# First attention of a two-layer kernel: the swap of k's halves issued by ScalarE, and another order of work on TensorE

## The chip, the core and the metric

The kernel runs on one core of a Trainium2 chip. The metric is the device time of one execution in microseconds (us), lower is better. The kernel before takes 1952.88 us (median of three runs, 1952.42 to 1953.05).

## What is computed

The reference is a two-layer transformer over 32 samples of 256 tokens with 128 channels. Only the first attention is touched by the change:

```python
h = _layernorm(x, axis=-1) * (1 + ca) + sa
x = x + ga * _L0_attn_ref(h, norm_w, Wq, Wkv, Wout, q_gamma, k_gamma)
...
# inside _L0_attn_ref, for each sample: 16 query heads and 8 key heads of 64
x = _rmsnorm(tokens, norm_w)
q = (x @ Wq).reshape(b, n, QH, DH).transpose(0, 2, 1, 3)
kv = x @ Wkv
...
q = _mh_rmsnorm(q, q_gamma)
k = _mh_rmsnorm(k, k_gamma)
sim = jnp.einsum('bhgid,bhjd->bhgij', q, k)
sim = jnp.tanh(sim / SOFTCLAMP) * SOFTCLAMP
sim = sim * DH ** (-0.5)
sim = jnp.where(causal, neg, sim)
attn = jax.nn.softmax(sim, axis=-1)
out = jnp.einsum('bhgij,bhjd->bhid', attn, v)
```

Behind it come a mixture of experts, a second attention and a gated network. They are the same in both kernels.

## The kernel before, in words

`build` runs five stages one after another: `setup`, `attention0`, `moe`, `attention1`, `mlp`. `attention0` is one loop over samples, written as a software pipeline: iteration n holds the attention of sample n, the normalising of q and k of sample n+1, the projections of sample n+2 and the layer norm of sample n+3. Each of the five engines has its own list of calls for an iteration, in an order written out by hand, and engines meet only through semaphores that count finished calls (`s_qg` counts the `dve_gain` calls, six for a sample; `s_ks` the copies of k, two; `s_k2` the landed swaps of k, 16 for a transfer). An engine takes its calls strictly in the written order, so a call that waits holds up all that stand behind it.

The calls of one sample on TensorE (PE), with the names that the rows use:

- **projections** `pe_project_qk` (L448), six calls m = 0 to 5 of 512 columns in f32, m = 2 and 5 giving k; `pe_values` (L411), two calls of the same size. Three PSUM banks `pW[0..2]` are shared by projections, values, transposes and the output projection; the tables `QK_BANK`, `QT_BANK`, `KT_BANK` and others say which call writes which bank, and the waits at the head of a call say whose reading of that bank must be over.
- **turns of k and q** `pe_turn_k` (L466, t = 0, 1) and `pe_turn_q` (L490, i = 0 to 3), eight f16 transposes each.
- **score products** `pe_score` (L513), 48 calls in f16, 256 columns each, twelve for each of four groups g of heads. q and k are split into a high and a low f16 half that lie in the two halves of the partitions. Odd calls use `k2`, which is k with its halves swapped, even calls use `k1`. `pe_score(n, 0, 0)` waits for `s_k2`; the call m = 0 of each group also waits until the tanh of the group before has read the score banks `pS` (`s_th`).
- **weighing** `pe_weigh` (L533, L535), 48 calls of 66 columns in f32, twelve for each group. The first of a group waits for the mask (`s_mk`).
- **heads back** `pe_heads_back` (L551, eight f32 transposes), **output projection** `pe_out_project` (L563, four calls of 256 columns in f32), `pe_out_back` (L581) and `pe_transpose_x` (L396), two transposes each.

An f32 product is two MATMUL records of the trace, an f16 product or a transpose is one.

On ScalarE (ACT): `act_tanh` and `act_exp` (L1001, L1009) for each group, `act_square_qk` (L965) for each of the six projections, `act_take_k` (L985) two copies of k out of PSUM into `k1`, and smaller calls. On VectorE (DVE): `dve_gain` (L794), which multiplies a projection out of PSUM by gamma and so frees its bank, `dve_sums`, `dve_factors`, `dve_norm`, `dve_outputs`, `dve_take_q` (L874). On GpSimd (POOL): the causal masks (L1083), sums and two low halves. For each projection, square on ACT comes first and gain on DVE behind it (`dve_gain` waits for `s_sq`).

SyncE (SP) issues all transfers. In iteration n of its own loop it waits until both copies of k of sample n are there, and issues the two transfers that swap the halves (L378, L379) and behind them the load of a row of modulations for sample n+3 (L365). In iteration 1 it also issues all the loads of later weights.

Of the kernel before, what the change touches and what calls it, by code (L numbers as in the profile page):

```python
# [14 lines left out]
P = 128  # L15
# [281 lines left out]
def attention0(nc, c, weights, later, following):  # L297
# [3 lines left out]
    with ExitStack() as ctx:  # L301
# [87 lines left out]
        def pe_transpose_x(pe, n, t):  # L389
            if not 0 <= n < B:  # L390
                return
            if t == 0:
                pe.wait_ge(s_hm, 2 * n + 2)
                if n >= 1:
                    pe.wait_ge(s_qg, 6 * n - 2)
# [4 lines left out]
        def pe_values(pe, n, t):  # L400
# [3 lines left out]
            if t == 0:  # L404
                if n + 1 < B:
                    pe.wait_ge(s_qg, 6 * n + 7)
                else:
                    pe.wait_ge(s_qg, 6 * n + 4)
            else:
                pe.wait_ge(s_va, 2 * n + 1)  # L410
            pe.matmul(pW[V_BANK[t]][:, :], hT[n % 2][:, t * P:(t + 1) * P], wkv[:, KW:2 * KW], start=True, stop=True).then_inc(s_v, 1)  # L411

        def pe_project_qk(pe, n, m):
# [3 lines left out]
            if m == 0:  # L417
                pe.wait_ge(s_hT, n + 1)
            elif m == 1:
                if n >= 2:  # L420
                    pe.wait_ge(s_qs, 4 * n - 5)
                elif n >= 1:
                    pe.wait_ge(s_qg, 6 * n - 1)
            elif m == 2:
                if n >= 1:
# [3 lines left out]
            elif m == 3:  # L429
                if n >= 1:  # L430
                    pe.wait_ge(s_qs, 4 * n - 3)
                else:
                    pe.wait_ge(s_qg, 6 * n + 3)
            elif m == 4:
                if n >= 1:
                    pe.wait_ge(s_qs, 4 * n - 2)
                else:
                    pe.wait_ge(s_qg, 6 * n + 2)
# [11 lines left out]
        def pe_turn_k(pe, n, t):  # L450
# [3 lines left out]
            if t == 0:  # L454
                if n + 1 < B:
                    pe.wait_ge(s_qg, 6 * n + 9)
                else:
                    pe.wait_ge(s_va, 2 * n + 2)
            else:
                if n + 1 < B:  # L460
                    pe.wait_ge(s_qg, 6 * n + 8)
                else:
                    pe.wait_ge(s_qs, 4 * n - 1)
# [5 lines left out]
        def pe_turn_q(pe, n, i):  # L469
# [4 lines left out]
            if i == 0:  # L474
                pe.wait_ge(s_ks, 2 * n + 1)
            elif i == 1:
                pe.wait_ge(s_ks, 2 * n + 2)
            elif i == 2:
                if n + 1 < B:
                    pe.wait_ge(s_qg, 6 * n + 11)  # L480
                else:
                    pe.wait_ge(s_qs, 4 * n + 2)
            else:
                if n + 1 < B:
                    pe.wait_ge(s_qg, 6 * n + 12)
                else:
                    pe.wait_ge(s_st, 3 * n - 5)
# [51 lines left out]
        def pe_heads_back(pe, n, t, j):  # L539
# [3 lines left out]
            if j == 0:  # L543
                if t == 0:
                    if n + 1 < B:
                        pe.wait_ge(s_qs, 4 * n + 8)
                    else:
                        pe.wait_ge(s_st, 3 * n - 2)
                else:
                    pe.wait_ge(s_at, 2 * n + 1)  # L550
# [4 lines left out]
        def pe_out_project(pe, n, j):  # L555
            if not 0 <= n < B:
                return
            if j == 0:
# [3 lines left out]
                pe.wait_ge(s_at, 2 * n + 2)  # L562
# [12 lines left out]
        def pe_out_back(pe, n, t):  # L575
            if not 0 <= n < B:
                return
            if t == 0:
                pe.wait_ge(s_og, n + 1)
                pe.wait_ge(s_og, n + 1)  # L580
# [5 lines left out]
        def _(pe):  # L586
            pe_spread_first_rows(pe)
            pe.wait_ge(s_prep, 2)
            for n in range(-3, B + 2):
                for m in range(4, 8):  # L590
                    pe_score(pe, n, 1, m)
                    pe_weigh(pe, n - 1, 3, m + 1)
                pe_score(pe, n, 1, 8)
                pe_score(pe, n, 1, 9)
                pe_weigh(pe, n - 1, 3, 9)
                pe_score(pe, n, 1, 10)
                pe_score(pe, n, 1, 11)
                pe_weigh(pe, n - 1, 3, 10)
                pe_turn_q(pe, n, 3)
                pe_weigh(pe, n - 1, 3, 11)  # L600
                pe_values(pe, n + 1, 0)
                pe_weigh(pe, n, 0, 0)
                pe_project_qk(pe, n + 2, 1)
                pe_weigh(pe, n, 0, 1)
                pe_score(pe, n, 2, 0)
                pe_weigh(pe, n, 0, 2)
                pe_score(pe, n, 2, 1)
                pe_weigh(pe, n, 0, 3)
                pe_score(pe, n, 2, 2)
                pe_heads_back(pe, n - 1, 0, 0)  # L610
                pe_heads_back(pe, n - 1, 0, 1)
                pe_score(pe, n, 2, 3)
                pe_heads_back(pe, n - 1, 0, 2)
                pe_heads_back(pe, n - 1, 0, 3)
                pe_weigh(pe, n, 0, 4)
                pe_score(pe, n, 2, 4)
                pe_weigh(pe, n, 0, 5)
                pe_values(pe, n + 1, 1)
                pe_weigh(pe, n, 0, 6)
                pe_score(pe, n, 2, 5)  # L620
                pe_weigh(pe, n, 0, 7)
                pe_score(pe, n, 2, 6)
# [4 lines left out]
                pe_score(pe, n, 2, 7)  # L627
                pe_heads_back(pe, n - 1, 1, 1)
                pe_score(pe, n, 2, 8)
                pe_heads_back(pe, n - 1, 1, 2)  # L630
                pe_score(pe, n, 2, 9)
                pe_heads_back(pe, n - 1, 1, 3)
                pe_score(pe, n, 2, 10)
                pe_weigh(pe, n, 0, 8)
                pe_weigh(pe, n, 0, 9)
# [11 lines left out]
                pe_out_project(pe, n - 1, 2)  # L647
                pe_weigh(pe, n, 1, 2)
                pe_score(pe, n, 3, 0)
# [1828 lines left out]
```

## Time and profile before

| | |
|---|---|
| median of three runs | 1952.88 us |
| the profiled execution, its own time | 1955.93 us |
| its span, first to last instruction | 1954.2 us |
| busy: PE, DVE, ACT, POOL | 97%, 81%, 74%, 35% |
| `attention0`, by the first and last copy of its turned input | from about 19 us to about 917 us |

The page of the profile has the share of each engine over the span and the span in 40 slices. The timeline gives, for one engine, start and duration of instructions (neighbours of one kind are merged, with their count), and behind them in brackets the idle time before and what ended it. MATMUL records overlap: the time from the start of one call to the start of the next is what a call costs TensorE. The view of windows gives the busy time of each engine in chosen stretches, and the granted clock.

### The profile page before, as it was taken

The numbers are of one execution on the slowest core, as the hardware profiler recorded it, in microseconds if no ns is written. First come the engines' busy times: TensorE is split into PE (matmuls) and PEld (weight loads), VectorE is DVE, ScalarE is ACT, GpSimd is POOL, SyncE is SP. The second block draws the span as 40 slices with busy tenths as digits, with TensorE's granted clock in tenths as the row PEclk, the third lists the DMA queues.
The fourth block names the chain that finished last, engine by engine and source line by source line (L and its number), as shares of the span: only waits on it lengthen the run. The fifth ranks groups of instructions, "written<-read, shape, count | busy, mean of one in ns | idle before, by whom it ended". The sixth has DMA issues, their size and how long they took to land. (4 is left out here: it accounts for less than half of the span.)

```text
span 1954.2 us, 41236 instructions
## 1 busy us (share of the span) xinstructions
PE 1891.4 (97%) x14878; PEld 1323.5 (68%) x14878; DVE 1588.3 (81%) x3865; ACT 1443.6 (74%) x2020; POOL 674.2 (35%) x956
## 2 busy tenths in 40 slices
PE   7999999999999999998899999899999978999998
PEld 4788888888888888887344444677777753444443
DVE  6888888888888888873776775699999977888886
ACT  3888888888888888884677777466767755666665
POOL 1555555555555555552000000255555540000000
PEclk7999999999999999998999999899999999999999
DMA  2501111011110111100675554100000000000000
GB/s 96 127 22 28 29 28 28 15 28 29 29 28 15 29 28 29 26 23 1 138 174 119 111 120 99 45 2 2 2 3 2 2 2 6 12 11 17 12 17 17
DMA packets 57001, 75.67 MB, mean 39 GB/s; under 512 B 9456, under 2 KB 34144, under 8 KB 56672
## 3 DMA queue, kind: packets, MB, share of 16 engines
q1 hardware_dynamic: 56800, 73.03, 15.7%
q8 instruction: 122, 2.00, 0.4%
q14 instruction: 79, 0.65, 0.1%
HBM read 51.47 MB, written 4.77 MB: 29 GB/s over the span
## 5 line engine op out<-in xcount | busy, mean ns | idle before, releaser
L513 PE MATMUL a_pS<-qs,k 128*128 128x256 f16 x1536 | 377.2, 273 | 3.7 <-issue 2.6
L533 PEld LDWEIGHTS a_pO<-va,pr 128*128 128x128 f32 x2048 | 322.9, 192 | 82.1 <-issue 72.9
L533 PE MATMUL a_pO<-va,pr 128*128 128x66 f32 x2048 | 332.3, 252 | 3.1 <-DVE on L857 2.5
L1083 POOL TENSOR_SCALAR_AFFINE_SELECT pr<-pr 128x512 f32<-128x512 f32 x256 | 181.7, 734 | 192.4 <-ACT pr L1009 192.3
L1001 ACT ACTIVATE th<-a_pS 128x1536 f32<-128x1536 f32 x128 | 185.8, 1451 | 68.1 <-PE a_pS L513 65.2
L1982 ACT ACTIVATE c_pr<-c_pS 128x2048 f32<-128x2048 f32 x96 | 180.4, 1879 | 59.8 <-PE c_pS L1785 59.8
L2026 POOL TENSOR_SCALAR_AFFINE_SELECT c_pr<-c_pr 128x512 f32<-128x512 f32 x256 | 155.5, 638 | 181.9 <-DVE c_pr L1875 181.9
L513 PEld LDWEIGHTS a_pS<-qs,k 128*128 128x128 f16 x1536 | 196.3, 131 | 7.3 <-issue 4.0
L864 POOL TENSOR_TENSOR qp<-qg,qp 128x1024 f16<-128x1024 f32 x64 | 149.2, 2331 | 121.5 <-ACT qp L977 121.5
L1009 ACT ACTIVATE pr<-th 128x1536 f32<-128x1536 f32 x128 | 189.6, 1481 | 1.1
L535 PEld LDWEIGHTS a_pO<-va,pr 128*128 128x128 f32 x1024 | 162.5, 192 | 31.4 <-issue 28.7
L535 PE MATMUL a_pO<-va,pr 128*128 128x66 f32 x1024 | 175.9, 254 | 0.0
L1292 PE MATMUL b_pD<-b_a,b_dn 128*128 128x512 f32 x320 | 165.3, 602 | 4.3 <-DVE b_a L1442 3.9
L1282 PE MATMUL b_pU<-b_hT,b_un 128*128 128x512 f32 x320 | 163.8, 597 | 0.0
L1442 DVE TENSOR_TENSOR b_a<-b_q,b_cwB 128x512 f32<-128x512 f32 x128 | 87.8, 689 | 73.0 <-ACT b_q L1533 59.1
L1094 POOL TENSOR_TENSOR as<-on 128x128 f32<-128x128 f32 x256 | 115.6, 457 | 87.7 <-DVE on L857 86.3
L1520 ACT ACTIVATE b_r<-b_pU 128x512 f32<-128x512 f32 x160 | 95.6, 598 | 67.8 <-PE b_pU L1282 67.8
L448 PE MATMUL a_pW<-a_wq,hT 128*128 128x512 f32 x256 | 139.6, 629 | 1.5 <-DVE qg L794 1.5
L1875 DVE TENSOR_SCALAR c_pr<-c_pr 128x2048 f32<-128x2048 f32 x96 | 116.4, 1212 | 28.2 <-ACT c_pr L1982 28.2
L874 DVE COPY qs<-a_pW 128x1024 f16<-128x1024 f16 x128 | 88.3, 690 | 58.2 <-PE a_pW L490 58.1
L965 ACT ACTIVATE sq<-a_pW 128x512 f32<-128x512 f32 x192 | 114.4, 596 | 24.6 <-PE a_pW L448 21.7
L794 DVE TENSOR_TENSOR qg<-a_pW,a_gam 128x512 f32<-128x512 f32 x192 | 125.9, 682 | 2.9 <-ACT sq L965 2.8
(267 smaller groups left out, 4336.2 us busy)
## 6 DMA issues: line engine op xcount, KB each, us to landing
b_cwB<-b_by_expert SPq DMA_DIRECT2D x64, 512.0 KB, 8.5
k<-k SPq DMA_DIRECT2D x64, 256.0 KB, 3.7
x<-in_L_attn_tokens_dram SPq DMA_DIRECT2D x8, 512.0 KB, 6.9
out_dram<-x SPq DMA_DIRECT2D x16, 256.0 KB, 2.3
mb<-a_by_sample SPq DMA_DIRECT2D x31, 128.0 KB, 3.5
d_h<-in_L_ffn_h_w_dram SPq DMA_DIRECT2D x2, 1024.0 KB, 8.2
c_gb<-c_by_sample SPq DMA_DIRECT2D x1, 2048.0 KB, 8.3
b_by_expert<-b_cwT SPq DMA_DIRECT2D x64, 8.0 KB, 1.4
```

The source lines that it names most:

```text
L448: pe.matmul(pW[QK_BANK[m]][:, :], hT[n % 2][:, t * P:(t + 1) * P], w, start=True, stop=True).then_inc(s_qk, 1)
L513: last = pe.matmul(out, (k1, k2)[part][k][:, h // G2, keys * P:(keys + 1) * P], q, start=part == 0, stop=part == 1)
L533: last = pe.matmul(out, w[:, hh * N + t * P:hh * N + (t + 1) * P], v[:, 0, p, :], start=True, stop=t == 0)
L535: last = pe.matmul(out, w[:, HPG * N + hh * P:HPG * N + (hh + 1) * P], v[:, 1, p, :], start=False, stop=True)
L864: eng.tensor_tensor(to[:, t, :, DH:2 * DH], x.rearrange('p (h d) -> p h d', d=DH), to[:, t, :, 0:DH], ALU.subtract).then_inc(done, 1)
L1001: act.activation(th[:, :], pS[:, :], ACT.Tanh, scale=1.0 / SOFTCLAMP).then_inc(s_th, 1)
L1009: act.activation(pr[g % 2][:, :], th[:, :], ACT.Exp, scale=SOFTCLAMP * DH ** (-0.5)).then_inc(s_pr, 1)
L1083: last = gp.affine_select(out=own, in_=own, compare_op=ALU.is_ge, fill=0.0, base=0, pattern=[[0, HPG], [1, P]], channel_multiplier=-1)
L1282: pe.matmul(pU[(IT * n + u) % 4][:, :], uT[:, t, :], hT[n % 3][:, :], start=True, stop=True).then_inc(s_up, 1)
L1292: pe.matmul(pD[:, :], dT[:, t * D:(t + 1) * D], a[(IT * n + u) % 4][:, :], start=u == 0, stop=u == IT - 1).then_inc(s_dn, 1)
L1982: act.activation(pr[(3 * n + b) % NB][:, :, :], pS[:, :, :], ACT.Exp, scale=float(1.0 / np.sqrt(np.float32(DQ)))).then_inc(s_ex, 1)
L2026: gp.affine_select(out=part, in_=part, compare_op=ALU.is_ge, fill=0.0, base=0, pattern=[[0, HPG], [1, P]], channel_multiplier=-1).then_inc ...
```

## The change

The two swap transfers leave SP and are issued by ScalarE (`act_swap_k`), behind its own copies of k and ahead of `act_exp(n, 2)`. SP keeps the row loads, released by the same count of `s_ks`. All four engines get another order of calls within the iteration; the calls themselves, their number and their operands stay the same. The bank tables and with them the waits of the bank users change. The diff, cut:

```diff
-        QK_BANK = (1, 0, 1, 1, 0, 2)
+        QK_BANK = (1, 0, 1, 2, 1, 2)
         QT_BANK = (1, 0, 0, 2)
-        KT_BANK, V_BANK, HB_BANK = (1, 0), (1, 1), (2, 2)
-        X_BANK, O_BANK, BACK_BANK = 1, 2, 2
+        KT_BANK, V_BANK, HB_BANK = (0, 2), (0, 1), (2, 1)
+        X_BANK, O_BANK, BACK_BANK = 0, 2, 0
...
             for n in range(B):
-                k = n % 2
-                if n >= 2:
-                    sp.wait_ge(s_sc, 4 * (n - 1))
                 sp.wait_ge(s_ks, 2 * n + 2)
-                sp.dma_start(k2[k][0:DH, :, :], k1[k][DH:P, :, :]).then_inc(s_k2, 16)
-                sp.dma_start(k2[k][DH:P, :, :], k1[k][0:DH, :, :]).then_inc(s_k2, 16)
                 if n + 3 < B:
                     sp_load_rows(sp, n + 3)
...
         def pe_project_qk(pe, n, m):
...
             elif m == 3:
                 if n >= 1:
+                    pe.wait_ge(s_ks, 2 * n)
+            elif m == 4:
+                if n >= 1:
                     pe.wait_ge(s_qs, 4 * n - 3)
...
             else:
-                if n >= 3:
-                    pe.wait_ge(s_st, 3 * n - 8)
-                elif n >= 2:
-                    pe.wait_ge(s_qs, 4 * n - 4)
-                elif n >= 1:
-                    pe.wait_ge(s_qg, 6 * n)
+                pe.wait_ge(s_qg, 6 * n + 4)
...
+                    pe_score(pe, n, 2, m)
+                    pe_weigh(pe, n, 0, m + 1)
                 pe_score(pe, n, 2, 11)
-                pe_weigh(pe, n, 0, 10)
                 pe_project_qk(pe, n + 2, 2)
-                pe_weigh(pe, n, 0, 11)
...
                 pe_out_project(pe, n - 1, 0)
+                pe_out_project(pe, n - 1, 1)
+                pe_out_project(pe, n - 1, 2)
+                pe_out_project(pe, n - 1, 3)
                 pe_weigh(pe, n, 1, 0)
-                pe_out_project(pe, n - 1, 1)
+                pe_score(pe, n, 3, 0)
                 pe_weigh(pe, n, 1, 1)
...
                 pe_turn_k(pe, n + 1, 0)
-                pe_score(pe, n, 3, 2)
-                pe_weigh(pe, n, 1, 6)
-                pe_score(pe, n, 3, 3)
+                for m in range(1, 6):
+                    pe_score(pe, n, 3, m)
+                    pe_weigh(pe, n, 1, m + 1)
...
                 pe_turn_k(pe, n + 1, 1)
-                pe_score(pe, n, 3, 4)
+                pe_score(pe, n, 3, 6)
                 pe_weigh(pe, n, 1, 7)
...
                 pe_turn_q(pe, n + 1, 0)
+                pe_score(pe, n, 3, 7)
+                pe_out_back(pe, n - 1, 0)
+                pe_weigh(pe, n, 1, 8)
                 pe_score(pe, n, 3, 8)
-                pe_out_back(pe, n - 1, 0)
+                pe_out_back(pe, n - 1, 1)
+                pe_weigh(pe, n, 1, 9)
                 pe_score(pe, n, 3, 9)
+                pe_project_qk(pe, n + 2, 3)
+                pe_weigh(pe, n, 1, 10)
                 pe_score(pe, n, 3, 10)
-                pe_out_back(pe, n - 1, 1)
+                pe_weigh(pe, n, 1, 11)
...
                 pe_turn_q(pe, n + 1, 1)
                 pe_score(pe, n, 3, 11)
-                pe_weigh(pe, n, 1, 10)
-                pe_project_qk(pe, n + 2, 3)
-                pe_weigh(pe, n, 1, 11)
                 pe_project_qk(pe, n + 2, 4)
                 pe_project_qk(pe, n + 2, 5)
...
                 pe_weigh(pe, n, 2, 0)
-                for m in range(0, 3):
-                    pe_score(pe, n + 1, 0, m)
-                    pe_weigh(pe, n, 2, m + 1)
-                pe_score(pe, n + 1, 0, 3)
+                pe_score(pe, n + 1, 0, 0)
...
+                pe_score(pe, n + 1, 0, 11)
                 pe_project_qk(pe, n + 3, 0)
...
                 pe_weigh(pe, n, 3, 0)
-                pe_weigh(pe, n, 3, 1)
-                pe_score(pe, n + 1, 1, 0)
-                pe_weigh(pe, n, 3, 2)
-                pe_score(pe, n + 1, 1, 1)
-                pe_weigh(pe, n, 3, 3)
-                pe_score(pe, n + 1, 1, 2)
-                pe_score(pe, n + 1, 1, 3)
-                pe_weigh(pe, n, 3, 4)
+                pe_turn_q(pe, n + 1, 2)
+                pe_turn_q(pe, n + 1, 3)
+                for m in range(0, 11):
+                    pe_score(pe, n + 1, 1, m)
+                    pe_weigh(pe, n, 3, m + 1)
+                pe_score(pe, n + 1, 1, 11)
+                pe_values(pe, n + 2, 0)
+                pe_heads_back(pe, n, 0, 0)
+                pe_values(pe, n + 2, 1)
+                pe_weigh(pe, n + 1, 0, 0)
+                pe_score(pe, n + 1, 2, 0)
...
                 lower(dve, n + 1, 0, 1, s_lo)
                 dve_sums(dve, n + 2, 0)
                 dve_ln(dve, n + 3, 0)
                 dve_take_q(dve, n + 1, 0)
                 dve_add(dve, n - 1)
+                dve_outputs(dve, n, 2)
+                dve_ln(dve, n + 3, 1)
+                dve_gain(dve, n + 2, 3)
+                dve_measure(dve, n - 1, 1)
                 dve_take_q(dve, n + 1, 1)
-                dve_measure(dve, n - 1, 1)
+                dve_outputs(dve, n, 3)
+                dve_gain(dve, n + 2, 4)
+                dve_mean_square(dve, n + 2)
...
+        def act_swap_k(act, n):
+            if not 0 <= n < B:
+                return
+            k = n % 2
+            act.wait_ge(s_ks, 2 * n + 2)
+            act.dma_start(k2[k][0:DH, :, :], k1[k][DH:P, :, :]).then_inc(s_k2, 16)
+            act.dma_start(k2[k][DH:P, :, :], k1[k][0:DH, :, :]).then_inc(s_k2, 16)
...
                 act_gate(act, n - 1)
+                act_hi(act, n + 1, 1, 1)
                 act_take_k(act, n + 1, 0)
                 act_take_k(act, n + 1, 1)
+                act_swap_k(act, n + 1)
                 act_exp(act, n, 2)
+                act_square_qk(act, n + 2, 3)
                 act_tanh(act, n, 3)
-                act_square_qk(act, n + 2, 3)
                 act_square_qk(act, n + 2, 4)
                 act_square_qk(act, n + 2, 5)
                 act_exp(act, n, 3)
                 act_square_h(act, n + 3, 0)
                 act_turned(act, n + 3)
+                act_square_h(act, n + 3, 1)
+                act_tanh(act, n + 1, 0)
+                act_exp(act, n + 1, 0)
+                act_square_qk(act, n + 3, 0)
```

## Rows read from the trace of the kernel before

**Rows 1.** The page: busy time of each engine, share of the span, instructions.

```profile
PE 1891.4 (97%) x14878; PEld 1323.5 (68%) x14878; DVE 1588.3 (81%) x3865; ACT 1443.6 (74%) x2020; POOL 674.2 (35%) x956
```

**Rows 2.** A window of one iteration: length, busy time by engine, clock, DMA share.

```profile
391.78:418.64 26.86, 26.86 (x232) 22.66 (x230) 23.09 (x55) 23.09 (x31) 15.22 (x21) 1.00 0.10 26
```

**Rows 3.** Timeline of SyncE: start, duration, transfer; samples 3, 13 and 28.

```profile
121.93 0.46 SPq L378 DMA_DIRECT2D k<-k  x1
...
391.78 0.46 SPq L378 DMA_DIRECT2D k<-k  x1
392.29 0.60 SPq L379 DMA_DIRECT2D k<-k  x1
392.93 0.59 SPq L365 DMA_DIRECT2D mb<-a_by_sample  x1
...
795.59 0.46 SPq L378 DMA_DIRECT2D k<-k  x1
```

**Rows 4.** Line L379, the second swap transfer: duration ns, and us to landing.

```profile
L379 SPq DMA_DIRECT2D k<-k x32: 585/597/599, 46.5 to 875.3; - x32
...
DMA to landing us min/median/max: 3.7/3.8/4.5
```

**Rows 5.** Timeline of TensorE from k's second turn to the next sample's first score.

```profile
389.96 0.61 PE L466 MATMUL a_pW<-id,kp 128*128 128x128 f16 x8
390.41 0.27 PE L513 MATMUL a_pS<-qs,k 128*128 128x256 f16 x1
...
393.99 0.33 PE L535 MATMUL a_pO<-va,pr 128*128 128x66 f32 x2
394.16 1.07 PE L448 MATMUL a_pW<-a_wq,hT 128*128 128x512 f32 x2
395.07 1.02 PE L448 MATMUL a_pW<-a_wkv,hT 128*128 128x512 f32 x2
395.93 0.33 PE L533 MATMUL a_pO<-va,pr 128*128 128x66 f32 x2
396.12 0.27 PE L513 MATMUL a_pS<-qs,k 128*128 128x256 f16 x1
```

**Rows 6.** Timeline of TensorE, a late start of that same score product.

```profile
288.25 0.27 PE L513 MATMUL a_pS<-qs,k 128*128 128x256 f16 x1 [0.52 <-issue]
```

**Rows 7.** Timeline of TensorE: weighing twice in a row, and output projections.

```profile
411.05 0.34 PE L535 MATMUL a_pO<-va,pr 128*128 128x66 f32 x2
411.22 0.39 PE L533 MATMUL a_pO<-va,pr 128*128 128x66 f32 x2
411.44 0.27 PE L513 MATMUL a_pS<-qs,k 128*128 128x256 f16 x1
...
412.80 0.65 PE L563 MATMUL a_pW<-at,a_wo 128*128 128x256 f32 x2
413.29 0.33 PE L533 MATMUL a_pO<-va,pr 128*128 128x66 f32 x2
```

**Rows 8.** Timeline of ScalarE from the copies of k to the third group's tanh.

```profile
389.77 1.94 ACT L985 ACTIVATE k<-a_pW 128x1024 f16<-128x1024 f16 x2 [0.42 <-PE a_pW L466]
391.60 1.49 ACT L1009 ACTIVATE pr<-th 128x1536 f32<-128x1536 f32 x1
393.17 1.45 ACT L1001 ACTIVATE th<-a_pS 128x1536 f32<-128x1536 f32 x1
394.52 0.59 ACT L965 ACTIVATE sq<-a_pW 128x512 f32<-128x512 f32 x1
```

**Rows 9.** Timelines of VectorE and GpSimd: gain, q's copy, statistics, masks.

```profile
393.00 0.69 DVE L874 COPY qs<-a_pW 128x1024 f16<-128x1024 f16 x1
393.61 0.47 DVE L136 BATCH_NORM_STATS2 stat<-x 128x6 f32<-128x128 f32 x2
400.35 0.68 DVE L794 TENSOR_TENSOR qg<-a_pW,a_gam 128x512 f32<-128x512 f32 x1
403.19 1.23 POOL L1083 TENSOR_SCALAR_AFFINE_SELECT pr<-pr 128x512 f32<-128x512 f32 x2 [2.22 <-ACT pr L1009]
```

More of the change, by code:

```diff
@@ L393, in pe_transpose_x @@
                 pe.wait_ge(s_hm, 2 * n + 2)
-                if n >= 1:
-                    pe.wait_ge(s_qg, 6 * n - 2)
+                if n >= 2:
+                    pe.wait_ge(s_qs, 4 * n - 6)
+                elif n >= 1:
+                    pe.wait_ge(s_qg, 6 * n - 4)
             last = pe.transpose(pW[X_BANK][:, t * P:(t + 1) * P], hm[:, t, :], c.id32[:, :])
@@ L404, in pe_values @@
             if t == 0:
+                if n >= 1:
+                    pe.wait_ge(s_qs, 4 * n - 1)
+                else:
+                    pe.wait_ge(s_hT, n + 2)
+            else:
                 if n + 1 < B:
@@ L407, in pe_values @@
                 else:
-                    pe.wait_ge(s_qg, 6 * n + 4)
-            else:
-                pe.wait_ge(s_va, 2 * n + 1)
+                    pe.wait_ge(s_qg, 6 * n + 5)
             pe.matmul(pW[V_BANK[t]][:, :], hT[n % 2][:, t * P:(t + 1) * P], wkv[:, KW:2 * KW], start=True, stop=True).then_inc(s_v, 1)
@@ L417, in pe_project_qk @@
             if m == 0:
-                pe.wait_ge(s_hT, n + 1)
+                if n >= 1:
+                    pe.wait_ge(s_qg, 6 * n - 1)
             elif m == 1:
-                if n >= 2:
-                    pe.wait_ge(s_qs, 4 * n - 5)
+                if n >= 1:
+                    pe.wait_ge(s_va, 2 * n - 1)
+                else:
+                    pe.wait_ge(s_hT, n + 1)
+            elif m == 2:
+                if n >= 3:
+                    pe.wait_ge(s_at, 2 * n - 4)
                 elif n >= 1:
-                    pe.wait_ge(s_qg, 6 * n - 1)
-            elif m == 2:
-                if n >= 1:
                     pe.wait_ge(s_va, 2 * n)
@@ L455, in pe_turn_k @@
                 if n + 1 < B:
[L456 to L460, printed above, removed]
                     pe.wait_ge(s_qg, 6 * n + 8)
                 else:
-                    pe.wait_ge(s_qs, 4 * n - 1)
+                    pe.wait_ge(s_va, 2 * n + 1)
+            else:
+                if n >= 2:
+                    pe.wait_ge(s_og, n - 1)
+                elif n >= 1:
+                    pe.wait_ge(s_qs, 4 * n)
+                else:
+                    pe.wait_ge(s_qg, 6 * n + 6)
             out = pW[KT_BANK[t]][:, :].bitcast(F16)
@@ L474, in pe_turn_q @@
             if i == 0:
-                pe.wait_ge(s_ks, 2 * n + 1)
+                if n + 1 < B:
+                    pe.wait_ge(s_qg, 6 * n + 9)
+                else:
+                    pe.wait_ge(s_at, 2 * n - 2)
             elif i == 1:
-                pe.wait_ge(s_ks, 2 * n + 2)
+                if n >= 2:
+                    pe.wait_ge(s_st, 3 * n - 5)
+                else:
+                    pe.wait_ge(s_ks, 2 * n + 1)
             elif i == 2:
-                if n + 1 < B:
-                    pe.wait_ge(s_qg, 6 * n + 11)
+                if n + 2 < B:
+                    pe.wait_ge(s_hT, n + 3)
                 else:
@@ L486, in pe_turn_q @@
                 else:
-                    pe.wait_ge(s_st, 3 * n - 5)
+                    pe.wait_ge(s_ks, 2 * n + 2)
             out = pW[QT_BANK[i]][:, :].bitcast(F16)
@@ L547, in pe_heads_back @@
                     else:
-                        pe.wait_ge(s_st, 3 * n - 2)
+                        pe.wait_ge(s_og, n)
                 else:
-                    pe.wait_ge(s_at, 2 * n + 1)
+                    if n + 2 < B:
+                        pe.wait_ge(s_va, 2 * n + 6)
+                    elif n + 1 < B:
+                        pe.wait_ge(s_qs, 4 * n + 5)
+                    else:
+                        pe.wait_ge(s_at, 2 * n)
             last = pe.transpose(pW[HB_BANK[t]][:, j * P:(j + 1) * P], as_[:, t, j * P:(j + 1) * P], c.id32[:, :])
@@ L579, in pe_out_back @@
                 pe.wait_ge(s_og, n + 1)
-                pe.wait_ge(s_og, n + 1)
+                if n + 2 < B:
+                    pe.wait_ge(s_ks, 2 * n + 5)
+                elif n + 1 < B:
+                    pe.wait_ge(s_qs, 4 * n + 7)
+                else:
+                    pe.wait_ge(s_st, 3 * n - 2)
             last = pe.transpose(pW[BACK_BANK][:, t * P:(t + 1) * P], og[:, t * P:(t + 1) * P], c.id32[:, :])
@@ L701, in _ @@
                     keep_busy(pe, c, pS, (4, 7)[n + 3])
-                for m in range(6, 12):
+                pe_weigh(pe, n, 2, 3)
+                for m in range(3, 11):
                     pe_score(pe, n + 1, 0, m)
-                    pe_weigh(pe, n, 2, m - 1)
-                pe_weigh(pe, n, 2, 11)
-                pe_turn_q(pe, n + 1, 2)
+                    pe_weigh(pe, n, 2, m + 1)
+                pe_score(pe, n + 1, 0, 11)
                 pe_project_qk(pe, n + 3, 0)
@@ L1115, in _ @@
             for n in range(-3, B + 2):
+                gp_mask(gp, n - 1, 2, 1)
+                gp_sum(gp, n - 1, 1)
                 gp_modulate(gp, n + 2, 1)
```

134 lines of the change are left out of this document (43 added, 91 removed).

## The prediction

> **What bounds the kernel now.** I read the page first: TensorE is busy nearly all the time [rows 1]. In a window of one iteration of the first attention it is busy without a gap, at a granted clock of 1.00, which is the 2.4 GHz level, while VectorE and ScalarE each have 3.8 us to spare [rows 2]. Then SyncE's timeline: the first swap transfer is issued once for each sample, so sample 3 to sample 28 gives the mean length of an iteration, (795.59 - 121.93) / 25 = 26.95 us [rows 3]. The quiet window has 26.86.
>
> Then TensorE's own timeline, for the steps from one start to the next. A score product costs 0.11 us, an eight-fold turn 0.45 [rows 5], a weighing 0.17 behind a score, but 0.22 behind another weighing [rows 7], since its weights then had no long product to be loaded behind. A 512-column product costs 0.91 behind a weighing and 0.86 behind another projection [rows 5]. An output projection behind a weighing costs 0.49 [rows 7]; it has half the columns. With these steps the old order sums to 48 scores x 0.109 = 5.23, six turns x 0.448 = 2.69, twelve single f32 transposes x 0.109 = 1.31, 48 weighings 8.44, eight large products 7 x 0.912 + 0.858 = 7.24, four output projections x 0.486 = 1.94: 26.86 us. That is the quiet iteration to 0.01 us (third digits are those of the records behind the rows), so in it TensorE's issue is the bound.
>
> There is a second bound beside it. The swap is issued at 391.78, the second transfer at 392.29 lands 3.7 to 3.8 us later [rows 3, 4], at about 396.03, and the first score of the next sample starts at 396.12 [rows 5]. In another iteration that score starts only after 0.52 us of idle [rows 6]; the landing takes up to 4.5 us [rows 4]. So k's swap sets the time in the bad iterations, and the 0.09 us between 26.86 and 26.95 is that.
>
> **TensorE's sum after the change.** The diff gives the new order; nothing is added or removed in it. (a) Seven large products that stood behind a weighing or a turn now stand behind a score, a transpose or a projection. No row shows a projection behind a score. The near row is a weighing behind a score, which saves the same 0.05 as behind a projection [rows 7]; so I take 0.054 x 7 = 0.38, with 0 as the other end. (b) The four output projections stand in a row behind a projection: 0.431 for 0.486, 0.22 in all, by the same 0.055 that a projection saves behind another; 0 is the other end. (c) Three weighings behind a weighing and one behind a turn now follow scores or transposes: 0.20. In sum 26.86 - 0.80 = 26.06 us, if nothing waits.
>
> **What waits.** I lay ScalarE's and VectorE's new orders against TensorE's, with E the end of k's second turn (390.41 in the old trace [rows 5]).
>
> - The copy of k starts at E + 0.20, since 0.04 passes between the recorded end of a turn and the copy, and takes 1.02 (two copies that overlap by 0.10 fill 1.94): E + 1.22 [rows 5, 8].
> - ScalarE waits for its own copy and issues two transfers. From the end of the copy at 391.71 to the end of the second issue at 392.89, SyncE needs 1.18 us [rows 3, 8]. ScalarE has issued no transfer in this trace. I take the same 1.18, and as bounds 0 (the issue runs beside the engine's work) and 1.77 (SyncE's row load, released by the same semaphore, gets in between with its own 0.59 [rows 3]). E + 2.40.
> - `act_exp(n, 2)`: 0.05 to start, 1.49, E + 3.94. The square of projection 3, moved ahead of the tanh, starts 0.10 before that end and takes 0.60, as behind the tanh in the old order [rows 8]: E + 4.44.
> - `dve_gain(n+2, 3)`: 0.05 and 0.68 [rows 9], E + 5.17. VectorE is free by then.
> - Projection 5 now writes the bank of projection 3 (`QK_BANK` 2 and 2) and so waits for `s_qg` 6n + 4, that gain. It starts 0.11 behind it, E + 5.28.
>
> TensorE alone would be at projection 5 at E + 4.34 (13 short calls of 1.73 in sum, two turns 0.90, projections 3 and 4 1.72). It loses 0.94, and 0.05 more since the weights of a product that waited are loaded in the open. The iteration becomes 26.06 + 0.99 = 27.05 us. In the old order projection 5 waited for an addition long done (`s_st`): this chain is new.
>
> Other new waits lie under it. The mask of group 2 is done at E + 3.94 + 0.05 + 1.23 [rows 9] = 5.22 and is wanted at 6.19. The tanh of group 3, behind the square, ends at E + 4.34 + 1.45 = 5.79, wanted by the next sample's first score at E + 6.36. The q copy on VectorE, behind the gain and the statistics (0.47 and 0.69 [rows 9]), ends at E + 6.2: nearly tight. The swap: 0.07 from copy to issue, 0.51 to the second issue and 3.74 to its landing, 0.09 to the product [rows 3 to 5, 8], so E + 1.22 + 4.41 = 5.63, which leaves 0.7 us. So the late landings are hidden too, and 27.05 compares with the mean 26.95, not with the quiet 26.86. The first output call of group 2 on VectorE comes late, behind the gain of projection 4 and a reduction, at about E + 10.1, wanted at 10.6.
>
> SyncE's row load no longer queues behind the swap and starts 1.1 us earlier; nobody waits for it near. On GpSimd the masks move by one place; it has 11 us of idle in an iteration [rows 2].
>
> **The sum.** Some 28 full iterations x (27.05 - 26.95) = +2.8 us. The first and last iterations, where little work covers a chain, get the 1.18 of ScalarE's issue once or twice: +1, estimated. The difference, about +4, is made on the profiled execution (1955.93, span 1954.2) and is put on the median, which is 3 us lower: 1952.9 + 4 = 1957.
>
> **Rivals.** (1) The issue costs ScalarE nothing. Then exp, square and gain are done before TensorE is at projection 5 (E + 5.28 - 1.18 = 4.10 against 4.34), and the next limit is the landing: E + 5.63 against 5.37 for the first score, 26.06 + 0.26 = 26.32 us. Saved: 28 x 0.63 = 17.6 us, 1935; the row load now moves its 128 KB beside the swap and late landings count again, which takes some of it back: 1938. For it: the transfers are handled by the sequencer, not by the engine's pipe. Against it: SyncE's sequencer is held 0.46 and 0.60 us by the same two instructions [rows 3], and ScalarE takes its list in order. The Trainium skill, "Advanced Engine Details and Errata", section "Sequencer and Instruction Queues", says that other engine instructions can be read and queued while the sequencer's microcode works on a control instruction; if this covers a transfer, this rival is the case. No row here shows it.
>
> (2) Both issuers get in each other's way. SyncE and ScalarE are released by the same count, and the row load's 0.59 falls between ScalarE's two: 27.05 + 0.59 = 27.64, + 28 x 0.69 = 19 and 1: 1973, slower. It decides from the first 0.1 us of holding up on, since the chain has no slack. For it: the two issues on one queue already stretch from 0.46 to 0.60 [rows 3]. Against it: they are small transfers, and nobody else issues at that moment in the old trace, so none shows it. The Trainium skill, "Perfetto Trace Analysis", section "DMA Instruction — HWDGE (DVE, Sync)", says that the descriptor generator is locked for exclusive use by the instruction it works for; if SP and ACT share one, this is what happens.
>
> (3) The cheaper steps don't come: a projection behind a score costs 0.91 as before, and output projections in a row 0.49. Of the 0.60 of (a) and (b), 0.11 lies before projection 5 and is absorbed in its wait; 0.49 x 28 = 14 us come on top of my forecast: 1970, slower. For it: no row has that neighbourhood. Against it: the weighings' rows [rows 7].
>
> **Chances.** The forecast, a chain through ScalarE's issue that eats what TensorE's order saves: 0.42, own range 1953 to 1964. Rival 1: 0.28. Rival 2: 0.20. Rival 3: 0.10. A measurement of this kernel tells about 0.2% (3.9 us) from no change. Faster by more: rival 1, 0.27. Within: the lower half of the forecast and a rest of rival 1, 0.21. Slower by more: 0.52. The range that leaves out some 2 in 10 runs from 1937 to 1975.
>
> **What would show it.** In the profile after, ScalarE's queue has two transfers of about 0.5 us between the second copy of k and the exp, and the exp starts 1.2 us behind the copy; `dve_gain` ends about 5.2 us behind the turn and projection 5 starts 0.1 us behind it, with idle time of about 0.9 us on TensorE in each iteration and PE's share down to 96% there; swaps are issued 27.05 us apart. If the exp starts right behind the copy, rival 1 holds and the first score starts 0.09 us behind the landing. If ScalarE's second issue lasts over 1 us, it is rival 2. A projection step of 0.91 behind a score is rival 3. I am wrong altogether if VectorE or GpSimd, whose orders I followed only at the waits named, hold TensorE elsewhere.

## The result, and the profile after

The changed kernel takes 1980.2 us (median of four runs, 1979.85 to 1985.55) against 1952.65: ratio 1.0148, 95% interval 1.0130 to 1.0165. It is slower, as forecast, but by 27.5 us and not by 4, and the time lies 5 us above the range.

The profiled execution after has a span of 1978.1 us, 23.9 more than before. The page, to be laid beside [rows 1]:

```profile
PE 1874.3 (95%) x14878; PEld 1300.7 (66%) x14878; DVE 1572.9 (80%) x3865; ACT 1432.9 (72%) x2020; POOL 684.0 (35%) x956
...
q10 hardware_dynamic: 5120, 16.78, 3.3%
```

TensorE does the same instructions in 17 us less busy time, but it idles 41 us more (103.8 of the span's 1978.1 us, 62.8 of 1954.2 before). A second DMA queue, q10, is there: ScalarE's. ScalarE's timeline over one swap, with SyncE's beside it (start, duration, what, and in brackets the idle time before), answers to [rows 3, 8]:

```profile
432.37 1.02 ACT L974 ACTIVATE k<-a_pW 128x1024 f16<-128x1024 f16 x1 [0.35 <-PE a_pW L464]
433.42 0.47 ACTq L981 DMA_DIRECT2D k<-k  x1
433.92 0.61 ACTq L982 DMA_DIRECT2D k<-k  x1
434.64 1.49 ACT L1006 ACTIVATE pr<-th 128x1536 f32<-128x1536 f32 x1 [1.25 <-issue]
436.03 0.58 ACT L954 ACTIVATE sq<-a_pW 128x512 f32<-128x512 f32 x1
...
433.41 0.32 SPq L365 DMA_DIRECT2D mb<-a_by_sample  x1
```

The exp stands 1.25 us behind the copy while the two issues run: ScalarE's list stops for them, and so it does in all 23 iterations from 130 to 760 us (28.9 us of wait, 1.25 each). And SyncE's row load now goes out at the same moment as the first swap transfer. VectorE and TensorE in the same iteration, to be laid beside [rows 5, 9]:

```profile
436.64 0.69 DVE L783 TENSOR_TENSOR qg<-a_pW,a_gam 128x512 f32<-128x512 f32 x1 [1.81 <-ACT sq L954]
...
432.17 0.27 PE L517 MATMUL a_pS<-qs,k 128*128 128x256 f16 x1
...
435.65 1.02 PE L444 MATMUL a_pW<-a_wq,hT 128*128 128x512 f32 x2
437.48 1.10 PE L444 MATMUL a_pW<-a_wkv,hT 128*128 128x512 f32 x2 [0.80 <-DVE qg L783]
438.41 0.33 PE L537 MATMUL a_pO<-va,pr 128*128 128x66 f32 x2
438.92 0.27 PE L517 MATMUL a_pS<-qs,k 128*128 128x256 f16 x1 [0.18 <-issue]
```

The reader is to see two waits in one iteration. Projection 5 (437.48) starts behind the gain that ends at 437.33, and the next sample's first score (438.92) starts 0.51 behind the weighing at 438.41, where 0.17 would do. The first wait was forecast, the second was not: the second transfer, issued at 433.92, lands 4.91 us later, and the score starts 0.09 us behind that landing. The view of line L982 has, against 3.8 in [rows 4]:

```profile
L982 ACTq DMA_DIRECT2D k<-k x32: 469/615/615, 44.4 to 902.1; - x32
...
DMA to landing us min/median/max: 3.7/5.1/10.0
```

From the swap of sample 3 (128.65) to that of sample 28 (821.16) an iteration takes 27.70 us in the mean, 26.95 before. One iteration is far longer, that from sample 1's swap (66.56) to sample 2's (101.04): 34.5 us against 26.9. SyncE's timeline at its start, TensorE's first score of sample 1, and the window behind it (length, busy time of PE, PEld, DVE, ACT, POOL, granted clock, DMA share, GB/s):

```profile
66.92 13.45 SPq L146 DMA_DIRECT2D x<-in_L_attn_tokens_dram  x6
...
77.12 0.37 PE L517 MATMUL a_pS<-qs,k 128*128 128x256 f16 x1 [5.23 <-issue]
...
77.12:81.27 4.15, 4.15 (x23) 4.15 (x24) 0.79 (x3) 0.67 (x3) 0.10 (x1) 0.50 1.19 290
```

In iteration 1 SyncE's list has, behind the row load, six loads of 512 KB of the tokens of later samples (L146) and only then the loads of later weights. They now go out beside sample 1's swap, where before they queued behind it on SyncE, and that swap lands 10.0 us behind its second issue, at 77.03. The first load of weights is issued at 80.42, so what meets this swap are the row load and the token loads. The first score waits 5.2 us for the landing. Behind that idle time the granted clock is 0.50, the level of 1.2 GHz, until 81.27: a score and a weighing together take 0.54 us there and not 0.28, which makes about 2.1 us more, an estimate from half of the 4.15 us.

### The profile page after: what moved, and what is told of

Its sections match the earlier page's. It is cut to its first block and busy times, and to the rows that moved or that the text cites. A ratio compares the mean times of both kernels' runs of the same rounds, so it can differ in the third digit from the quotient of the medians.

```text
span 1978.1 us, 41237 instructions
## 1 busy us (share of the span) xinstructions
PE 1874.3 (95%) x14878; PEld 1300.7 (66%) x14878; DVE 1572.9 (80%) x3865; ACT 1432.9 (72%) x2020; POOL 684.0 (35%) x956
## 5 line engine op out<-in xcount | busy, mean ns | idle before, releaser
L517 PE MATMUL a_pS<-qs,k 128*128 128x256 f16 x1536 | 417.1, 274 | 21.1 <-issue 17.0
L537 PEld LDWEIGHTS a_pO<-va,pr 128*128 128x128 f32 x2048 | 315.3, 192 | 63.2 <-issue 58.4
L537 PE MATMUL a_pO<-va,pr 128*128 128x66 f32 x2048 | 325.5, 250 | 2.9 <-POOL pr L1081 2.5
L517 PEld LDWEIGHTS a_pS<-qs,k 128*128 128x128 f16 x1536 | 223.2, 145 | 26.0 <-issue 23.8
L1081 POOL TENSOR_SCALAR_AFFINE_SELECT pr<-pr 128x512 f32<-128x512 f32 x256 | 156.3, 634 | 232.8 <-ACT pr L1006 232.8
L783 DVE TENSOR_TENSOR qg<-a_pW,a_gam 128x512 f32<-128x512 f32 x192 | 131.4, 685 | 101.3 <-ACT sq L954 101.3
L853 POOL TENSOR_TENSOR qp<-qg,qp 128x1024 f16<-128x1024 f32 x64 | 139.1, 2174 | 125.8 <-ACT qp L966 125.8
L1092 POOL TENSOR_TENSOR as<-on 128x128 f32<-128x128 f32 x256 | 162.2, 634 | 58.9 <-DVE on L846 57.8
L539 PE MATMUL a_pO<-va,pr 128*128 128x66 f32 x1024 | 172.7, 250 | 0.0
L539 PEld LDWEIGHTS a_pO<-va,pr 128*128 128x128 f32 x1024 | 158.1, 192 | 14.3 <-issue 14.3
L444 PE MATMUL a_pW<-a_wq,hT 128*128 128x512 f32 x256 | 131.6, 596 | 0.9 <-DVE qg L783 0.6
L2169 PE MATMUL d_pH<-d_a,d_h1T 128*128 128x512 f16 x512 | 121.3, 380 | 3.5 <-DVE d_a L2281 3.5
```

The lines of the kernel that those rows point to most:

```text
L517: last = pe.matmul(out, (k1, k2)[part][k][:, h // G2, keys * P:(keys + 1) * P], q, start=part == 0, stop=part == 1)
L537: last = pe.matmul(out, w[:, hh * N + t * P:hh * N + (t + 1) * P], v[:, 0, p, :], start=True, stop=t == 0)
L539: last = pe.matmul(out, w[:, HPG * N + hh * P:HPG * N + (hh + 1) * P], v[:, 1, p, :], start=False, stop=True)
L1081: last = gp.affine_select(out=own, in_=own, compare_op=ALU.is_ge, fill=0.0, base=0, pattern=[[0, HPG], [1, P]], channel_multiplier=-1)
L1092: gp.tensor_tensor(as_[:, :, p * DH:(p + 1) * DH], o[:, :, 0, :], o[:, :, 1, :], ALU.add).then_inc(s_as, 1)
L2169: last = pe.matmul(pH[o][:, :], weights[:, i, o * P:(o + 1) * P], a[:, i, part, :], start=i == 0 and part == 0, stop=i == HT - 1 and part ...
```

## The experiments

All runs are compared with the kernel before on the same chip. The table gathers what the profiled execution of each shows: the mean iteration (swaps of samples 3 to 28, over 25), the shortest one, the iteration from sample 1 to 2, and the median time from the first swap issue to the landing of the transfer that the next sample's scores wait for. The four last columns are us too. The first row has the medians of before beside the four groups of runs.

| kernel | time, us (ratio, 95%) | mean | shortest | 1 to 2 | landing |
|---|---|---|---|---|---|
| before | 1951.5 to 1952.7 | 26.95 | 26.85 | 26.9 | 4.28 |
| the change | 1980.2 (1.0130 to 1.0165) | 27.70 | 27.44 | 34.5 | 5.53 |
| rows_behind | 1958.3 (1.0022 to 1.0046) | 27.16 | 27.11 | 27.2 | 4.20 |
| later_behind | 1969.8 (1.0074 to 1.0116) | 27.51 | 27.39 | 27.1 | 5.42 |
| rows_early | 1959.0 (1.0025 to 1.0053) | 27.13 | 27.11 | 27.1 | 4.19 |
| few_rows | 1966.0 (1.0056 to 1.0086) | 27.14 | 27.11 | 33.9 | 4.19 |
| small_rows | 1969.7 (1.0076 to 1.0107) | 27.19 | 27.12 | 35.1 | 5.10 |
| old_order_act | 1991.9 (1.0186 to 1.0220) | 28.02 | 27.95 | 36.1 | 5.42 |
| sp_swap | 1941.2 (0.9930 to 0.9960) | 26.62 | 26.32 | 27.1 | 4.28 |
| sp_swap_m1 | 1931.1 (0.9877 to 0.9917) | 26.31 | 26.05 | 27.1 | 4.28 |
| sp_halves | 1922.9 (0.9837 to 0.9874) | 26.08 | 26.05 | 26.9 | 2.82 |
| before_m1 | 1947.9 (0.9972 to 0.9992) | 26.87 | 26.63 | 26.7 | 4.28 |

The theory formed from the trace after: of the 0.75 us that an iteration is longer, one part is the forecast wait at projection 5, the other is the late landing, and that is SyncE's row load meeting the swap on the DMA engines. The rivals: ScalarE's queue is slower by itself; or the new orders cost the time.

**rows_behind**: the row loads, and in iteration 1 the loads of tokens and weights, wait for the landed swap.

```diff
-                sp.wait_ge(s_ks, 2 * n + 2)
+                sp.wait_ge(s_k2, 32 * (n + 1))
```

> The changed kernel, but SyncE waits for the landed swap (s_k2) before it issues the row load and, for sample 1, the loads of later weights. Theory (the swap lands late because SyncE's row load is now issued beside it and shares the DMA engines): the second swap transfer lands 3.7 us behind its issue again instead of 5.0, the first score of a sample no longer waits for it, and only projection 5's wait of 1.05 us is left: iterations of 26.06 + 1.05 = 27.1 us instead of 27.7, and no long iteration behind sample 1; 1980 - 28 x 0.58 - 6 = 1957 to 1959 us. Rival (a transfer issued by ScalarE's queue lands later by itself): landing stays at 5.0 us and the time within 6 us of 1980, but for the long iteration.

Measured 1958.3 us. The landing is 4.20 us behind the first issue, so ScalarE's queue is not slow by itself. The view of waits of TensorE (who waited for whom, us in total, times, longest), from 130 to 760 us, first of the change, then of rows_behind:

```profile
PE a_pW L444 <- DVE qg L783: 18.6, 23, 0.9
PEld a_pS L517 <- issue: 12.5, 22, 1.7
```

```profile
PE a_pW L444 <- DVE qg L783: 18.7, 23, 1.0
PEld a_pS L517 <- issue: 0.9, 2, 0.5
```

Projection 5's wait stays at 0.81 us each time, the score's nearly goes. What is left, 27.11 us in undisturbed iterations, stands against the forecast's 27.05, and the whole time, 1958.3, against its 1957.

**later_behind**: in iteration 1 alone the row load and the loads behind it wait.

```diff
                 sp.wait_ge(s_ks, 2 * n + 2)
+                if n == 1:
+                    sp.wait_ge(s_k2, 32 * (n + 1))
```

> The changed kernel, but in its iteration 1 alone SyncE waits for the landed swap before the row load and the loads of later weights; all other row loads stay beside the swap. Theory (the iteration of 34.5 us behind sample 1 comes from the weights' loads overtaking the swap): that iteration goes back to 27 to 28.5 us, the others stay at 27.7; 1973 to 1975 us. Rival (the long iteration is the bandwidth that the weights take in either order, or the cold start): 1980 us.

Measured 1969.8, 10 us less than the change, where 5 to 7 were expected. The long iteration goes from 34.5 to 27.1, which is 7.4 us. The rest is that the mean of the others was 27.51 in this run and not 27.70, with fewer very late landings: the largest from sample 3 on is 5.7 us, where the change has 6.8, 6.7 and 6.3. What they go with is told in the last section.

The expectation spoke of the weights' loads overtaking the swap. The issue times above show that it is the token loads, and few_rows agrees: it has next to no row load beside this swap and still 33.9 us.

**old_order_act**: the kernel before with this part of the change alone.

```diff
-                sp.dma_start(k2[k][0:DH, :, :], k1[k][DH:P, :, :]).then_inc(s_k2, 16)
-                sp.dma_start(k2[k][DH:P, :, :], k1[k][0:DH, :, :]).then_inc(s_k2, 16)
...
                 act_take_k(act, n + 1, 1)
+                act_swap_k(act, n + 1)
```

> The kernel before with its old orders and banks, and only the transfers moved: ScalarE issues the two swap transfers behind its second copy of k, SyncE keeps the row loads, released by the copies. Theory (the landing, beside the row load, is 1.2 us later, and there the first score of the next sample already started 0.09 us behind the landing): iterations of about 28.1 us, 1953 + 28 x 1.15 + 6 = 1991 us. Rival (ScalarE has 3.8 us idle in an iteration and the issue goes into them, the change's loss comes from the new orders): 1953 to 1957 us.

Measured 1991.9. Moving the issue costs 40 us in the old orders, and 39 in the new ones (sp_swap, below, against the change). In the old orders the late landing does it, since that score had no slack, and 9 of the 40 us stand in the iteration from sample 1 to 2:

```profile
PE a_pS L508 <- DMA k<-k: 22.5, 23, 1.2
```

**sp_swap**: the other half alone, the new orders with SyncE issuing the swap.

```diff
                 sp.wait_ge(s_ks, 2 * n + 2)
+                sp.dma_start(k2[k][0:DH, :, :], k1[k][DH:P, :, :]).then_inc(s_k2, 16)
+                sp.dma_start(k2[k][DH:P, :, :], k1[k][0:DH, :, :]).then_inc(s_k2, 16)
...
-                act_swap_k(act, n + 1)
```

> The changed kernel with its new orders on all engines, but the two swap transfers issued by SyncE ahead of the row load, as in the kernel before; ScalarE issues none. Theory (ScalarE's 1.15 us of issue stand alone in the chain turn of k, copy, exp, square, gain, projection 5): TensorE no longer waits at projection 5, and the next limit is the landing, 0.26 us behind TensorE's own path: iterations of 26.32 us and some 0.1 for late landings, 1952.7 - 28 x 0.55 = 1937 us, faster than both. Rival (the new orders hold TensorE somewhere else once this wait is gone, or the bank of projection 5 alone costs the time): not under 1952 us, with TensorE still idle ahead of projection 5.

Measured 1941.2, faster than before; the rival that the orders themselves hold TensorE falls. The shortest iteration is 26.32, as worked out. The mean is 26.62, 0.2 more than expected: six landings in this execution took 4.9 to 5.7 us from the first issue, and each comes on top.

**sp_swap_m1** and **before_m1**: the wait for the landed swap stands before the second score product, the first that reads `k2`, in sp_swap and in the kernel before.

```diff
                 if g == 0:
                     pe.wait_ge(s_qs, 4 * n + 2)
-                    pe.wait_ge(s_k2, 32 * (n + 1))
...
+            if m == 1 and g == 0:
+                pe.wait_ge(s_k2, 32 * (n + 1))
```

> The kernel sp_swap (new orders, swap issued by SyncE) with the wait for the landed swap moved from the first to the second score product of a sample, the first that reads k2. Theory (in sp_swap the only steady wait of TensorE is for the landing, 0.26 us and more in late ones): one score and one weighing, 0.28 us, pass before the wait, so iterations go from 26.36 to about 26.1 us, and 1941 - 28 x 0.26 = 1934 us. Rival (another wait stands right behind, s_qs or s_th at the first score): within 2 us of 1941.

> The kernel before with only the wait for the landed swap moved to the second score product of a sample. Theory (before is bound by TensorE's order at 26.86 us and loses 0.1 us an iteration to late landings): 1951.5 - 2 to 3 = 1949 us, iterations of 26.86 to 26.9 us in the mean. Rival (the landing sets every iteration, since the first score always starts 0.09 us behind it): 28 x 0.28 = 8 us less, 1944 us.

Measured 1931.1, some 3 us better than expected, and 1947.9, 3.8 us less than before beside it. The first shows that the landing bound sp_swap in each iteration. The second shows how little it was in the kernel before: the mean went from 26.95 to 26.87, the median iteration from 26.89 to 26.84. There the first score started 0.09 us behind the landing in all iterations but the last; yet the records of its start give a wait of 0.1 us or less in most, and of 0.4 to 0.8 in four; all waits sum to 3.7 us, which is what before_m1 gained. So TensorE's order and the landing were all but equal bounds in before, and the prediction's reading, that the landing costs only in the bad iterations, is nearly right.

**sp_halves**: sp_swap with each transfer cut by heads.

```diff
-                sp.dma_start(k2[k][0:DH, :, :], k1[k][DH:P, :, :]).then_inc(s_k2, 16)
-                sp.dma_start(k2[k][DH:P, :, :], k1[k][0:DH, :, :]).then_inc(s_k2, 16)
+                for part, done in ((slice(0, KH // 2), s_k2), (slice(KH // 2, KH), s_k2b)):
+                    sp.dma_start(k2[k][0:DH, part, :], k1[k][DH:P, part, :]).then_inc(done, 16)
+                    sp.dma_start(k2[k][DH:P, part, :], k1[k][0:DH, part, :]).then_inc(done, 16)
...
                 elif g == 2:
                     pe.wait_ge(s_qs, 4 * n + 4)
+                    pe.wait_ge(s_k2b, 32 * (n + 1))
```

> The kernel sp_swap with each swap transfer cut in two: key heads 0 to 3, which groups 0 and 1 read, are swapped first, heads 4 to 7 by two more transfers with a count of their own, awaited at group 2. SyncE's queue holds four issues of about 0.5 us instead of two. Theory (landing bounds sp_swap, and it is half made of moving 512 KB): the first half lands about 1 us earlier, TensorE's order alone is left, iterations of 26.1 us without late ones, 1941 - 28 x (0.3 to 0.5) = 1928 to 1933 us. Rival (landing is a fixed latency and hardly depends on size): 1939 to 1943 us.

Measured 1922.9 us, the fastest version, 1.5% under the kernel before and 5 us under the range expected. The half that groups 0 and 1 read lands 2.82 us behind its first issue, and TensorE waits in no steady iteration (window of one iteration: length, busy time of PE, PEld, DVE, ACT, POOL, clock, DMA share):

```profile
404.00:430.07 26.07, 26.07 (x232) 21.99 (x229) 22.50 (x56) 22.77 (x31) 15.54 (x21) 1.00 0.11 26
```

That is the sum of the new order, 26.06, to 0.01 us, beside the old order's 26.86 in [rows 2]. The expectation's rival, a fixed latency, falls: half the size lands 1.46 us earlier.

**small_rows**, **few_rows**, **rows_early** ask what in the meeting costs. small_rows loads `mb[n % 3][:, 0, 0:32]` and few_rows `mb[n % 3][0:16, :, :]` from sample 4 on; rows_early releases the row load by the first copy of k, `s_ks` 2n + 1, and keeps the token and weight loads of iteration 1 behind the swap.

> The changed kernel, but from sample 4 on the row load beside the swap brings 128 bytes to a partition instead of 1024 (the rest of the modulation rows is left out, so the values are not the reference's). It tells apart why the swap lands 1.15 us later beside a row load. Theory A (bytes on the shared DMA engines): 128 packets that were of 1024 bytes and 59 ns, 0.47 us on each of the 16 engines, nearly vanish; what is left is the row load's place ahead: landing 4.3 to 4.5 us behind the first issue plus 0.2, iterations of 27.1 to 27.2 us, 1965 us. Theory B (a fixed price of a second transfer at the same moment: its descriptors are made and fetched first, whatever their size): landing stays at 5.3 us and more, iterations 27.5 to 27.7, 1977 to 1980 us.

> The changed kernel, but from sample 4 on the row load beside the swap goes to 16 of the 128 partitions, each with its full 1024 bytes (the other partitions keep old rows, so the values are not the reference's). small_rows had the same 128 packets with an eighth of the bytes and the swap still landed 5.1 us behind its first issue, where 4.2 is the time alone and 5.42 to 5.56 beside the full load. This run has an eighth of the bytes and of the packets. Theory A (each packet of the row load costs the swap's packets, whatever its size): landing 4.3 to 4.5 us, the first score's wait gone, iterations 27.1 us, 1966 us. Theory B (the price is one of place, the second transfer's descriptors start later behind another transfer that was issued at the same moment): landing 5.0 us as in small_rows, iterations 27.13 to 27.2 us.

> The changed kernel, but SyncE issues the row load behind the first copy of k (s_ks 2n + 1), about 1.9 us ahead of the swap, so that it is over when the swap's packets begin; the loads of later weights wait for the landed swap of sample 1. Same transfers, same sizes, same queues as in the change. Theory (only the meeting in time costs): landing back to 4.2 to 4.4 us behind the first issue, TensorE waits at projection 5 alone, iterations of 27.11 us, 1957 to 1959 us, as in rows_behind. Rival (two queues in use slow each other down even one after the other): landing near 5 us, 1967 us.

The issues by line, 300 to 600 us (target, queue, count, KB each, median us to landing, both transfers of a swap taken together, each from its own issue), small_rows first, then few_rows. The line of queue q1 in small_rows (packets, MB, share of the time of 16 engines) is for the last paragraph of this section:

```profile
k<-k ACTq DMA_DIRECT2D x22, 256.0 KB, 4.2
mb<-a_by_sample SPq DMA_DIRECT2D x11, 16.0 KB, 2.9
...
q1 hardware_dynamic: 1584, 0.18, 0.4%
```

```profile
k<-k ACTq DMA_DIRECT2D x22, 256.0 KB, 3.4
mb<-a_by_sample SPq DMA_DIRECT2D x11, 16.0 KB, 1.5
```

Both load 16 KB. As 128 packets of 128 bytes it makes the swap land at 5.10 us, as 16 packets of 1024 bytes at 4.19, the time alone. small_rows' time fell between its two expectations (1969.7), and its iterations, 27.19 in the mean and 27.12 the shortest, came near theory A's while its landing stayed near theory B's 5.3. The first score still started 0.09 us behind the landing in nearly all iterations, but waited less than 0.1 us in most iterations: 5.10 just uses up the slack. few_rows settles it for the number of packets. If the 128 packets are spread evenly over the 16 DMA engines, each gets eight, and 0.91 us is an estimated 0.11 us for each of them; full size adds 0.3 to 0.4 us in all. rows_early has the full load on the same queues, only earlier, and costs nothing: 4.19, 1959.0 us. So it is the number of packets under way at the same time, not the queue.

Where they meet is open. In small_rows a packet record of the row load lasts some 12 ns (0.4% of 16 engines' 300 us, over 1584), so eight of them fill 0.1 us of an engine's time, and the swap is late by 0.9. The 128 packets run from 0.94 to 2.45 us behind the swap's first issue at 128 bytes and from 0.95 to 2.69 at 1024, so it is not their size that sets their pace, and the swap's first packet already comes 0.2 to 0.4 us late. What feeds the packets to the engines may be the place as well as the engines themselves; no run tells these two apart.

## Why the prediction was right or wrong

**TensorE's sum: right.** All three cheaper steps, which no row of before showed, came. In the trace after a projection behind a score takes 0.432 + 0.429 us, an output projection in a row 0.431, and the whole order 26.06 or 26.07. Rival 3 falls.

**The chain through ScalarE's issue: right, step by step.** With E = 432.17: exp at E + 2.47 (forecast 2.45), square done at E + 4.44 (4.44), gain at E + 5.16 (5.17), projection 5 at E + 5.31 (5.28). Over 29 iterations, the steps from start to start show 0.97 us of wait and 0.075 of open weight loading for each, against 0.94 and 0.05 (the view of waits has 0.81 for the same wait, since records of neighbouring products overlap). rows_behind, where only this wait is left, has 27.11 for 27.05. The price of an issue on ScalarE, taken from SyncE's rows, was 0.47 and 0.61.

**The landing: wrong, and this is the step that failed.** The prediction put the swap at E + 5.63, with 3.74 us from the second issue to its landing, "which leaves 0.7 us", and said of SyncE's row load "nobody waits for it near". That price came from rows in which the row load stood behind the swap on the same queue. The change takes the swap out from ahead of it. Measured are 5.53 us from first issue to landing for 4.25, so the first score can start at E + 6.9 and not at E + 5.63: the slack of 0.7 is spent and 0.58 us in the mean are waited (16.4 us over 28 iterations). rows_behind, which only puts the row load (and the loads of iteration 1) behind the swap again, has 4.20 us and 1958.3, so it is this meeting that the prediction left out, and not the price of ScalarE's issue. The text had the effect in hand, but only inside rival 1, where the "128 KB beside the swap" took some of the gain back.

**The loads of iteration 1: left out.** The prediction followed SyncE's queue only as far as the row load. Behind it in iteration 1 stand the token loads and the loads of later weights, and the token loads now meet a swap: 34.5 us for 26.9. Of these 7.6 us some 5.3 are the wait for the landing, 2.1 the lower granted clock behind it, and 0.2 the forecast chain.

**Late landings: wrong way.** "The late landings are hidden too" needed the 0.7 of slack; with none they all count, and the mean lies 0.15 above the median (27.70 against 27.55). Even with the slack it held only in part: in rows_behind two landings of 5.6 us cost 0.5 each.

The sum of the profiled spans: up to sample 1's swap -1.6, iteration 1 to 2 +7.6, the 26 iterations to sample 28 +19.6 (26 x 0.75), the last three and the end of the stage -0.5, behind it -1.2: +23.9. The end of the stage is taken at its last addition to x, 916.8 us before and 941.9 after. In the 19.6, 26 x 0.16 = 4.2 belongs to the forecast chain and the rest, 15.4, to the landing. The forecast of +4 was thus the size of the one chain that it followed; that the kernel came out slower, as forecast, would have held by that chain alone.

**The rivals.** Rival 1 falls: the two issues hold the exp, which starts 0.11 us behind their end. The sentence of the Trainium skill in "Advanced Engine Details and Errata", section "Sequencer and Instruction Queues", does not cover a transfer on ScalarE, or the exp would not have stood for 1.25 us; the measurement decides. Rival 2 named the right partner and the wrong thing: the issues were not held up (0.32 us on SyncE, 0.47 and 0.61 on ScalarE, started within 0.01 us of each other), the landing was. The exclusive lock of the Trainium skill, "Perfetto Trace Analysis", section "DMA Instruction — HWDGE (DVE, Sync)", is not seen in these durations. The range was too narrow since both its upper cases kept the landing harmless.

## What to carry to other kernels

When a transfer changes its queue, look at what stood behind it: a queue was also what kept the others away from it, and they now start at its side. Price the landing with its new neighbours, not by the old row; count their packets rather than their bytes. And a transfer with several readers can be cut by who reads first; here that was worth 18 us beside the same orders (sp_swap to sp_halves), of which 10 were to be had by moving the wait alone to the first call that reads what lands (sp_swap_m1).

## What the runs showed of the hardware

- 128 packets of a DRAM to SBUF row load, issued by another engine at the same moment, delay a swap of 512 KB inside SBUF by 0.91 us at 128 bytes each and by 1.2 to 1.3 at 1024. By the packet records the swap's first packet comes 1.50 us behind its issue for 1.12 before, and its last one ends at 4.72 for 3.57. The Trainium skill, "DMA: Bandwidth & Descriptors", section "Queues, rings and completion order", says that a DMA engine takes turns between its queue rows packet by packet. A price by the packet fits that in kind, but the page counts several descriptors to a packet, and no run here shows that the records of the profile are its packets or that the turns are what costs the time.
- A transfer issued by ScalarE holds its list as long as it holds SyncE's: 1.11 us for the two, and the next instruction starts 0.11 us behind.
- The first half of a 512-column f32 projection takes 0.432 us behind a score or an f32 transpose (0.11 us each), 0.429 behind another projection, 0.484 behind a weighing or an f16 transpose, and 0.504 when it had waited for the gain.
- Very late landings go with packets of the queues q8 and q14, whose kind is "instruction". In sp_swap each of the six landings of 4.9 to 5.7 us has such a packet, of 0.5 to 1.2 us, beginning 2.6 to 3.2 us behind the first issue; the others, 4.24 to 4.33, have none that begins there. The five latest of the change (5.9 to 6.8) have one too. No run moved these packets, so this is read from the records and not tried.
- Behind 5.2 us of idle time TensorE's granted clock was 0.50 for the next 4.15 us of work (iteration from sample 1 to 2 of the change).
